# A recurrent layer on one core: R and H of x in one 256-column matmul, outputs in blocks of four pairs

## The chip, the core and the metric

The kernel runs on one core of one Trainium2 chip. A core has TensorE for matmuls, VectorE (DVE), ScalarE (ACT), GpSimd (POOL) and SyncE (SP, which here only starts transfers), and each runs its own list of instructions; semaphores order them. The metric is the device time of one launch in microseconds (us), the median of several runs.

## The reference

A gated recurrent layer over 512 time steps for a batch of 16, with 512 channels, all in fp32, and a residual:

```python
Xz = einsum(X, Wxz) + bxz;  Xr = einsum(X, Wxr) + bxr;  Xh = einsum(X, Wxh) + bxh
def step(H, xs):
    xz, xr, xh = xs
    Z = sigmoid(xz + H @ Whz.T + bhz)
    R = sigmoid(xr + H @ Whr.T + bhr)
    H_tilda = tanh(xh + R * H @ Whh.T + bhh)
    H_new = Z * H + (1.0 - Z) * H_tilda
    Y = H_new @ Whq.T + bhq
    return (H_new, Y)
_, Ys = scan(step, h0, (Xz, Xr, Xh))
return x + transpose(Ys, (1, 0, 2))
```

The flat input x of 16 x 512 x 512 is the sequence, cond_1024 is h0. Each step needs the state of the one before, so the steps can't be done side by side; the parts of x and the outputs Y can be done at any time.

## The kernel before

The steps go in 256 pairs `k`, each with a step `s` = 0 and 1 (the step's number is t = 2k + s). The batch is only 16, so a matmul's stationary side is the state (16 or 32 columns: one or both steps of the pair) and the weights stream past as the moving side, 128 columns in each matmul. TensorE's array is used as four column tiles of 32: tile `j` writes partitions 32j to 32j+31 of a PSUM bank and computes the output channels 128j to 128j+127. The 512 input channels are four parts `m`. So a product of a gate is 4 x 4 = 16 matmuls.

`recur` (L164) is the recurrent product of one gate g (R, Z or H) of one step; it adds onto what the bank `pre[k % 2]` has for that gate, one bank for each of R, Z and H. R and Z take the state, H takes R * state, for which it waits (`reset_ready`, in three parts); R waits for the state (`state_ready`, in three parts). `project_x` (L142) adds the part of x of one gate, for both steps of the next pair, and `project_y` (L153) the output of the pair before, 16 matmuls of 128 columns into `y_bank`. None of the two waits for the running step, so they are put behind Z and behind H, where TensorE would have to wait: they are the filler. The order is written out by hand in the loop at L201: R, Z, 4 matmuls of x's part, H, outputs of the pair before, 12 of x; then for the second step R, Z, 4 of x, H, 28 of x.

ACT fills a bank with the bias ahead of the products (`fill_pre` L232 for the three gates with one copy, `fill_y` L236). DVE transposes the products into the layout of the states (`turn` L267), ACT applies sigmoid or tanh, DVE multiplies and adds: `reset_state` L294, `kept` L299, `fresh` L305, the new `states` L309. After each pair DVE adds the output to the residual in `y_io` (`add_y` L271). SP loads x (`load_xt` L100) and the residual (`load_res` L103) for 8 pairs at a time and stores 8 pairs' outputs (L128), each 512 KB, with two buffers of each. All weights are loaded once, at the start.

Of the kernel before, what the change touches and what calls it, by code (L numbers as in the profile page):

```python
# [13 lines left out]
PAIRS = 8  # L14
TS = 2 * PAIRS
# [8 lines left out]
def gru(nc, x_t, x_res, h0, w_x, w_h, w_q, b_gate, b_out, out):  # L24
    tiles = x_t.shape[0]
    pairs = tiles * PAIRS

    with ExitStack() as ctx:
# [7 lines left out]
        wx = [sb(f"wx{g}", [P, G, C]) for g in range(3)]  # L36
# [4 lines left out]
        bias_out = sb("bias_out", [P, P])  # L41

        xt = sb("xt", [P, 2, PAIRS, G, Q])

        y_io = sb("y_io", [P, 2, PAIRS, P])

        states = sb("states", [P, 2, G, 3 * B])
# [11 lines left out]
        pre = [ctx.enter_context(nc.psum_tensor(f"pre{a}", [P, 3, 512], F32)) for a in range(2)]  # L59
# [3 lines left out]
        wx_loaded = [sem(f"wx_loaded{g}") for g in range(3)]  # L63
        wh_loaded = [sem(f"wh_loaded{g}") for g in range(3)]
        wq_loaded = sem("wq_loaded")
        bias_loaded = sem("bias_loaded")
        bias_ready = sem("bias_ready")
# [26 lines left out]
        def state_of(k, s):  # L94

            return states[:, (k + 1) % 2, :, 2 * B:3 * B] if s == 0 else states[:, k % 2, :, B:2 * B]

        @block.sync
        def _(sp):
            def load_xt(n):  # L100
                sp.dma_start(xt[:, n % 2], x_t[n]).then_inc(xt_loaded[n % 2], 16)

            def load_res(n):  # L103
                sp.dma_start(y_io[:, n % 2], x_res[n]).then_inc(y_loaded[n % 2], 16)

            load_xt(0)
            sp.dma_start(wx[R][:], w_x[R]).then_inc(wx_loaded[R], 16)
            for j in range(G):
                rows = slice(Q * j, Q * (j + 1))
                sp.dma_start(bias_in[rows].rearrange("p a g c -> p (a g c)"),  # L110
                             b_gate[j:j + 1].to_broadcast([Q, 6 * P])).then_inc(bias_loaded, 16)
                sp.dma_start(bias_out[rows], b_out[j:j + 1].to_broadcast([Q, P])).then_inc(bias_loaded, 16)  # L112
            sp.dma_start(wx[Z][:], w_x[Z]).then_inc(wx_loaded[Z], 16)
            sp.dma_start(wx[H][:], w_x[H]).then_inc(wx_loaded[H], 16)
            sp.wait_ge(zeroed, 2)
            sp.dma_start(states[:, 1, :, 2 * B:3 * B], h0).then_inc(h0_loaded, 16)  # L116
# [3 lines left out]
            load_res(0)  # L120
            load_xt(1)
            load_res(1)
            for n in range(tiles):
                if n + 2 < tiles:
                    sp.wait_ge(xt_used, n + 1)
                    load_xt(n + 2)
                sp.wait_ge(y_added, PAIRS * (n + 1))
                sp.dma_start(out[n], y_io[:, n % 2]).then_inc(stored[n % 2], 16)  # L128
                if n + 2 < tiles:
                    sp.wait_ge(stored[n % 2], 16 * (n // 2 + 1))  # L130
                    load_res(n + 2)
            for n in range(2):
                sp.wait_ge(stored[n], 16 * (tiles // 2))
# [7 lines left out]
        def _(pe):  # L141
            def project_x(k, g, first, end):  # L142

                n, tp = divmod(k, PAIRS)
                for m in range(first, end):
                    for j in range(G):
                        mm = nc.tensor.matmul(pre[k % 2][Q * j:Q * (j + 1), g, 0:P], xt[:, n % 2, tp, m, :],  # L147
                                              wx[g][:, m, P * j:P * (j + 1)], start=False, stop=(m == G - 1),
                                              skip_group_check=True)
                if tp == PAIRS - 1 and g == H and end == G:  # L150
                    mm.then_inc(xt_used, 1)

            def project_y(k):  # L153
                if k == 0:
                    pe.wait_ge(wq_loaded, 16)
                pe.wait_ge(y_filled, k + 1)
                for m in range(G):
                    for j in range(G):
                        mm = nc.tensor.matmul(y_bank[k % 2][Q * j:Q * (j + 1), 0:P], states[:, k % 2, m, B:3 * B],  # L159
                                              wq[:, m, P * j:P * (j + 1)], start=False, stop=(m == G - 1),  # L160
                                              skip_group_check=True)
                mm.then_inc(y_projected, 1)

            def recur(g, k, s):  # L164
                t = 2 * k + s
                if t == 0:
                    pe.wait_ge(wh_loaded[g], 16)
                for m in range(G):
# [7 lines left out]
                    else:  # L176
                        of = states[:, (k + 1) % 2, m, 2 * B:3 * B] if s == 0 else states[:, k % 2, m, 0:2 * B]
                    rows = B if s == 0 else 2 * B
                    for j in range(G):
                        mm = nc.tensor.matmul(pre[k % 2][Q * j:Q * j + rows, g, 0:P], of,  # L180
# [5 lines left out]
            pe.wait_ge(zeroed, 2)  # L186
            for a in range(2):
                for j in range(G):
                    for g in range(3):
                        nc.tensor.matmul(pre[a][Q * j:Q * (j + 1), g, 0:P], reset_state[:, 0, :],  # L190
                                         flat(reset_state[:]), start=True, stop=True)
                    mm = nc.tensor.matmul(y_bank[a][Q * j:Q * (j + 1), 0:P], reset_state[:, 0, :],
                                          flat(reset_state[:]), start=True, stop=True)
# [3 lines left out]
            for g in range(3):  # L197
                pe.wait_ge(wx_loaded[g], 16)
                project_x(0, g, 0, G)

            for k in range(pairs):  # L201
                more = k + 1 < pairs
                n, tp = divmod(k + 1, PAIRS)

                recur(R, k, 0)
                recur(Z, k, 0)
                if more:
                    if tp == 0:
                        pe.wait_ge(xt_loaded[n % 2], 16 * (n // 2 + 1))
                    pe.wait_ge(pre_filled, k + 2)  # L210
                    project_x(k + 1, R, 0, 1)
                recur(H, k, 0)
                if k > 0:
                    project_y(k - 1)
                if more:
                    project_x(k + 1, R, 1, G)

                recur(R, k, 1)
                recur(Z, k, 1)
                if more:  # L220
                    project_x(k + 1, Z, 0, 1)
                recur(H, k, 1)
                if more:
                    project_x(k + 1, Z, 1, G)
                    project_x(k + 1, H, 0, G)
            for h in range(N):
                pe.wait_ge(state_ready[h], 2 * pairs + 1)
            project_y(pairs - 1)

        @block.scalar  # L230
        def _(act):
            def fill_pre(k):  # L232

                nc.scalar.copy(pre[k % 2][:, :, 0:P], bias_rows[:]).then_inc(pre_filled, 1)  # L234

            def fill_y(k):  # L236
                if k >= 2:
                    act.wait_ge(y_added, k - 1)
# [131 lines left out]
```

## Time and profile before

| | us |
|---|---|
| median of 3 runs (2446.89 to 2451.39) | 2449.64 |
| the profiled execution | 2457.01 |
| its span | 2455.2 |
| TensorE matmul busy | 2351.4 (96%) |
| TensorE weight load busy | 2230.2 (91%) |
| DVE busy | 1345.5 (55%) |
| ACT busy | 817.1 (33%) |

The mean granted clock of TensorE is 0.998 of full speed (2.4 GHz). A record of TensorE is one row of the trace: each fp32 matmul of the code leaves two matmul records and two weight loads (PEld), 81984 of each. Matmul records overlap, since four column tiles work side by side, so their busy time tells only whether something was running. "L147" is line 147 of the kernel. "Idle before" is the time in which an engine did nothing before a row, with what ended it; "issue" means that nothing in the profile did. Two DMA queues carry instructions: q8 with 640 packets and q14 with 107.

| transfer | times | KB each | us to landing |
|---|---|---|---|
| xt from x | 32 | 512 | 3.4 |
| y_io from the residual | 32 | 512 | 3.3 |
| out from y_io | 32 | 512 | 2.8 |

### The profile page before, as it was taken

The page shows a single profiled execution, that of the slowest core. Times are in us where ns is not written, and L with a number is a line of the kernel's source. Part 1 is how long each engine was busy: PE and PEld are TensorE (multiplying, and loading weights), DVE is VectorE, ACT ScalarE, POOL GpSimd, SP SyncE. Part 2 cuts the span into 40 slices and gives each one's busy share as a digit, 9 for nine tenths or more (in the row PEclk, how much of TensorE's full clock was granted, in tenths as well). Part 3 has the DMA queues.
Part 4 walks back from the last instruction along what each step waited for, and adds up shares of the span by engine and source line. Part 5 has one row for each costly group of instructions (what it writes and reads, how often), then busy time and mean ns, then how long its engine had stood idle before and what let it go on. Part 6 is the DMA issues. An engine that isn't in the chain of part 4 may idle for free.

```text
span 2455.2 us, 177755 instructions
## 1 busy us (share of the span) xinstructions
PE 2351.4 (96%) x81984; PEld 2230.2 (91%) x81984; DVE 1345.5 (55%) x8961; ACT 817.1 (33%) x4610; POOL 0.8 (0%) x6
## 2 busy tenths in 40 slices
PE   8999999999999999999999999999999999999999
PEld 7999989999999999899999899989999898988898
DVE  3555555555555555555555555555555555555555
ACT  2333333333333333333333333333333333333333
POOL 0000000000000000000000000000000000000000
PEclk9999999999999999999999999999999999999999
DMA  4000000000000000000000100000000000000000
GB/s 165 30 22 22 22 30 30 30 13 22 30 30 30 13 30 22 30 30 13 30 22 30 30 23 21 22 30 30 30 13 22 30 30 30 13 22 30 30 13 13
DMA packets 16491, 69.53 MB, mean 28 GB/s; under 512 B 2304, under 2 KB 2432, under 8 KB 14848
## 3 DMA queue, kind: packets, MB, share of 16 engines
q1 hardware_dynamic: 15744, 58.17, 6.7%
q8 instruction: 640, 10.49, 1.8%
q14 instruction: 107, 0.88, 0.1%
HBM read 41.39 MB, written 16.78 MB: 24 GB/s over the span
## 4 chain that ended last, share of the span: by engine, by line
PE 95%; issue 4%; DMA 1%; SPq 0%; DVE 0%; ACT 0%
PE pre L180 57%; PE pre L147 29%; PE y_bank L159 9%; DMA wh<-in_w_hh 1%; SPq L110 0%; SPq L112 0%; DVE pre_t L269 0%; DVE fresh L305 0%; SPq L118 0%; DVE reset_state L294 0%; ACT cand L258 0%; SPq L116 0%; ACT z_not L254 0%; DVE states L309 0%; DVE kept L299 0%
## 5 line engine op out<-in xcount | busy, mean ns | idle before, releaser
L180 PE MATMUL pre<-wh,states 128*16 128x128 f32 x32768 | 1093.4, 273 | 22.7 <-issue 13.4
L147 PE MATMUL pre<-wx,xt 128*32 128x128 f32 x24576 | 1034.6, 273 | 67.9 <-issue 63.7
L269 DVE STREAM_TRANSPOSE pre_t<-pre 128x32 f32<-128x32 f32 (+2 forms) x3584 | 618.4, 216 | 801.8 <-PE pre L180 767.1
L180 PEld LDWEIGHTS pre<-wh,states 128*16 128x16 f32 x32768 | 949.9, 104 | 68.3 <-issue 60.8
L147 PEld LDWEIGHTS pre<-wx,xt 128*32 128x32 f32 x24576 | 814.3, 110 | 120.0 <-issue 117.2
L180 PE MATMUL pre<-wh,reset_state 128*16 128x128 f32 (+1 forms) x16384 | 616.8, 273 | 6.9 <-issue 5.5
L251 ACT ACTIVATE r_gate<-pre_t 128x16 f32<-128x16 f32 (+1 forms) x1536 | 234.5, 215 | 1003.1 <-DVE pre_t L269 1003.1
L180 PEld LDWEIGHTS pre<-wh,reset_state 128*16 128x16 f32 (+1 forms) x16384 | 473.0, 103 | 29.3 <-issue 27.8
L258 ACT ACTIVATE cand<-pre_t 128x16 f32<-128x16 f32 (+1 forms) x1536 | 234.8, 215 | 327.6 <-DVE pre_t L269 327.6
L159 PE MATMUL y_bank<-wq,states 128*32 128x128 f32 x8192 | 299.7, 273 | 1.5 <-DVE states L309 1.5
L159 PEld LDWEIGHTS y_bank<-wq,states 128*32 128x32 f32 x8192 | 258.0, 110 | 1.8 <-DVE states L309 1.8
L299 DVE TENSOR_TENSOR kept<-z_gate,states 128x64 f32<-128x64 f32 x512 | 115.5, 226 | 239.6 <-ACT z_gate L255 239.6
L305 DVE TENSOR_TENSOR fresh<-z_not,cand 128x16 f32<-128x16 f32 (+1 forms) x1536 | 223.1, 181 | 27.2
L294 DVE TENSOR_TENSOR reset_state<-r_gate,states 128x16 f32<-128x16 f32 (+1 forms) x1536 | 222.8, 182 | 27.4
L254 ACT ACTIVATE z_not<-pre_t 128x64 f32<-128x64 f32 x512 | 131.4, 257 | 293.5 <-DVE pre_t L269 293.5
L309 DVE TENSOR_TENSOR states<-fresh,kept 128x16 f32<-128x16 f32 (+1 forms) x1536 | 182.0, 174 | 0.0
L255 ACT ACTIVATE z_gate<-pre_t 128x64 f32<-128x64 f32 x512 | 122.7, 240 | 0.0
L234 ACT COPY pre<-bias_rows 128x384 f32<-128x384 f32 x256 | 120.9, 473 | 0.8 <-DVE bias_rows L280 0.8
L276 DVE TENSOR_TENSOR y_io<-y_bank,y_io 128x128 f32<-128x128 f32 x256 | 72.9, 285 | 1.4 <-PE y_bank L159 1.2
L239 ACT COPY y_bank<-bias_out 128x128 f32<-128x128 f32 x256 | 66.4, 259 | 0.0
L190 PE MATMUL pre<-reset_state 128*32 128x128 f32 x48 | 6.1, 361 | 1.3 <-POOL reset_state L138 1.3
L190 PEld LDWEIGHTS pre<-reset_state 128*32 128x32 f32 x48 | 5.1, 143 | 1.8 <-POOL reset_state L138 1.3
(11 smaller groups left out, 10.5 us busy)
## 6 DMA issues: line engine op xcount, KB each, us to landing
xt<-in_x_t SPq DMA_DIRECT2D x32, 512.0 KB, 3.4
y_io<-in_x_res SPq DMA_DIRECT2D x32, 512.0 KB, 3.3
out<-y_io SPq DMA_DIRECT2D x32, 512.0 KB, 2.8
wx<-in_w_xr SPq DMA_DIRECT2D x1, 1024.0 KB, 5.8
wx<-in_w_xz SPq DMA_DIRECT2D x1, 1024.0 KB, 6.0
wx<-in_w_xh SPq DMA_DIRECT2D x1, 1024.0 KB, 8.2
wh<-in_w_hr SPq DMA_DIRECT2D x1, 1024.0 KB, 11.0
wh<-in_w_hz SPq DMA_DIRECT2D x1, 1024.0 KB, 12.9
```

The lines of the kernel that those rows point to most:

```text
L147: mm = nc.tensor.matmul(pre[k % 2][Q * j:Q * (j + 1), g, 0:P], xt[:, n % 2, tp, m, :], wx[g][:, m, P * j:P * (j + 1)], start=False, stop=( ...
L159: mm = nc.tensor.matmul(y_bank[k % 2][Q * j:Q * (j + 1), 0:P], states[:, k % 2, m, B:3 * B], wq[:, m, P * j:P * (j + 1)], start=False, sto ...
L180: mm = nc.tensor.matmul(pre[k % 2][Q * j:Q * j + rows, g, 0:P], of, wh[g][:, m, P * j:P * (j + 1)], start=False, stop=(m == G - 1), skip_g ...
L234: nc.scalar.copy(pre[k % 2][:, :, 0:P], bias_rows[:]).then_inc(pre_filled, 1)
L251: nc.scalar.activation(r_gate[:, a:b], pre_t[R][:, a:b, mine], ACT.Sigmoid).then_inc(r_ready[h], 1)
L254: nc.scalar.activation(z_not[:], pre_t[Z][:, :, mine], ACT.Sigmoid, scale=-1.0)
L255: nc.scalar.activation(z_gate[:], pre_t[Z][:, :, mine], ACT.Sigmoid).then_inc(z_ready, 1)
L258: nc.scalar.activation(cand[:, a:b], pre_t[H][:, a:b, mine], ACT.Tanh).then_inc(cand_ready[h], 1)
L269: nc.vector.transpose(flat(pre_t[g][:, a:b]), pre[k % 2][:, g, Q * a:Q * b]).then_inc(done, 1)
L294: nc.vector.tensor_tensor(reset_state[:, a:b, B:2 * B], r_gate[:, a:b], old[:, a:b], ALU.mult).then_inc(reset_ready[h], 1)
L305: nc.vector.tensor_tensor(fresh[:, a:b], z_not[:, a:b], cand[:, a:b], ALU.mult).then_inc(fresh_ready[h], 1)
L309: nc.vector.tensor_tensor(new[:, a:b], fresh[:, a:b], kept[:, a:b], ALU.add).then_inc(state_ready[h], 1)
```

## The change

R and H of a pair now share one PSUM bank (`rh_bank`, R in columns 0 to 127 and H in 128 to 255), Z has its own (`z_bank`). `project_rh` computes x's parts of R and H with one matmul of 256 columns where there were two of 128; the weights lie side by side in `wx_rh`. `project_z` is the rest of `project_x`.

Outputs go by blocks of four pairs. `project_y(u, m)` gives each pair of block u a column tile of its own and streams all 512 columns of `wq` past each; in a pair of the next block one of the four parts `m` is done, 4 matmuls of 512 columns. For that `states` is a ring of 8 pairs. In the first four pairs there is no output work, and after the last pair four parts are left. The output add takes 256 columns at a time, in the first two steps of a block, between Z's transpose and `kept`. x, residual and output transfers go by four pairs, 256 KB each; xt's rows in memory are 512 bytes long where they were 4096. ACT fills the gates' banks with two copies, and `y_bank` once in four pairs with 512 columns. The order of the filler is also new, as the loop shows.

```diff
+            for u in range(2):
+                load_res(u)
+            for u in range(blocks):
+
+                if u + 2 < blocks:
+                    sp.wait_ge(xt_used, u + 1)
+                    load_xt(u + 2)
+                if u > 0:
+                    sp.wait_ge(y_added, 2 * u)
+                    sp.dma_start(out[u - 1], y_io[:, (u - 1) % 2]).then_inc(stored[(u - 1) % 2], 16)
+                    if u + 1 < blocks:
+                        sp.wait_ge(stored[(u - 1) % 2], 16 * ((u + 1) // 2))
+                        load_res(u + 1)
+            sp.wait_ge(y_added, 2 * blocks)
+            sp.dma_start(out[blocks - 1], y_io[:, (blocks - 1) % 2]).then_inc(stored[(blocks - 1) % 2], 16)
+            for half in range(2):
+                sp.wait_ge(stored[half], 16 * (blocks // 2))
 
...
-            def project_x(k, g, first, end):
-
-                n, tp = divmod(k, PAIRS)
+            def project_rh(k, first, end):
+
+                u, c = divmod(k, BLOCK)
                 for m in range(first, end):
                     for j in range(G):
-                        mm = nc.tensor.matmul(pre[k % 2][Q * j:Q * (j + 1), g, 0:P], xt[:, n % 2, tp, m, :],
-                                              wx[g][:, m, P * j:P * (j + 1)], start=False, stop=(m == G - 1),
-                                              skip_group_check=True)
-                if tp == PAIRS - 1 and g == H and end == G:
+                        mm = nc.tensor.matmul(rh_bank[k % 2][Q * j:Q * (j + 1), 0:2 * P], xt[:, u % 2, c, m, :],
+                                              wx_rh[:, m, j, :], start=False, stop=(m == G - 1), skip_group_check=True)
+                if end == G and c == BLOCK - 1:
                     mm.then_inc(xt_used, 1)
 
-            def project_y(k):
-                if k == 0:
-                    pe.wait_ge(wq_loaded, 16)
-                pe.wait_ge(y_filled, k + 1)
-                for m in range(G):
+            def project_z(k, first, end):
+                u, c = divmod(k, BLOCK)
+                for m in range(first, end):
                     for j in range(G):
-                        mm = nc.tensor.matmul(y_bank[k % 2][Q * j:Q * (j + 1), 0:P], states[:, k % 2, m, B:3 * B],
-                                              wq[:, m, P * j:P * (j + 1)], start=False, stop=(m == G - 1),
-                                              skip_group_check=True)
-                mm.then_inc(y_projected, 1)
-
-            def recur(g, k, s):
-                t = 2 * k + s
+                        nc.tensor.matmul(z_bank[k % 2][Q * j:Q * (j + 1), 0:P], xt[:, u % 2, c, m, :],
+                                         wx_z[:, m, P * j:P * (j + 1)], start=False, stop=(m == G - 1),
+                                         skip_group_check=True)
+
+            def project_y(u, m):
+
+                if m == 0:
+                    pe.wait_ge(y_filled, u + 1)
+                for c in range(BLOCK):
+                    mm = nc.tensor.matmul(y_bank[u % 2][Q * c:Q * (c + 1), :],
+                                          states[:, (u * BLOCK + c) % RING, m, B:3 * B], wq[:, m, :],
+                                          start=False, stop=(m == G - 1), skip_group_check=True)
+                if m == G - 1:
+                    mm.then_inc(y_projected, 1)
+
+            def recur(g, t):
+                k, s = divmod(t, 2)
...
             for k in range(pairs):
                 more = k + 1 < pairs
-                n, tp = divmod(k + 1, PAIRS)
-
-                recur(R, k, 0)
-                recur(Z, k, 0)
+                u, c = divmod(k, BLOCK)
+                recur(R, 2 * k)
+                recur(Z, 2 * k)
                 if more:
-                    if tp == 0:
-                        pe.wait_ge(xt_loaded[n % 2], 16 * (n // 2 + 1))
+                    if c == BLOCK - 1:
+                        pe.wait_ge(xt_loaded[(u + 1) % 2], 16 * ((u + 1) // 2 + 1))
                     pe.wait_ge(pre_filled, k + 2)
-                    project_x(k + 1, R, 0, 1)
-                recur(H, k, 0)
-                if k > 0:
-                    project_y(k - 1)
+                    project_z(k + 1, 0, 1)
+                recur(H, 2 * k)
+                if u > 0:
+                    if (u, c) == (1, 0):
+                        pe.wait_ge(wq_loaded, 16)
+                    project_y(u - 1, c)
                 if more:
-                    project_x(k + 1, R, 1, G)
-
-                recur(R, k, 1)
-                recur(Z, k, 1)
+                    project_rh(k + 1, 0, 1)
+
+                recur(R, 2 * k + 1)
+                recur(Z, 2 * k + 1)
                 if more:
-                    project_x(k + 1, Z, 0, 1)
-                recur(H, k, 1)
+                    project_z(k + 1, 1, 2)
+                recur(H, 2 * k + 1)
                 if more:
-                    project_x(k + 1, Z, 1, G)
-                    project_x(k + 1, H, 0, G)
+                    project_z(k + 1, 2, G)
+                    project_rh(k + 1, 1, G)
...
-            project_y(pairs - 1)
+            for m in range(G):
+                project_y(blocks - 1, m)
...
             def fill_pre(k):
 
-                nc.scalar.copy(pre[k % 2][:, :, 0:P], bias_rows[:]).then_inc(pre_filled, 1)
-
-            def fill_y(k):
-                if k >= 2:
-                    act.wait_ge(y_added, k - 1)
-                nc.scalar.copy(y_bank[k % 2][:, 0:P], bias_out[:]).then_inc(y_filled, 1)
+                nc.scalar.copy(rh_bank[k % 2][:, 0:2 * P], bias_rows[:, 0:2].rearrange("p g c -> p (g c)"))
+                nc.scalar.copy(z_bank[k % 2][:, 0:P], bias_rows[:, 2]).then_inc(pre_filled, 1)
+
+            def fill_y(u):
+                if u == 0:
+                    act.wait_ge(bias_out_loaded, 16)
+                if u >= 2:
+                    act.wait_ge(y_added, 2 * (u - 1))
+                nc.scalar.copy(y_bank[u % 2][:], bias_out[:]).then_inc(y_filled, 1)
...
+                if s == 1 and k + 2 < pairs:
+                    fill_pre(k + 2)
+                if s == 0 and k % BLOCK == BLOCK - 1:
+                    fill_y(k // BLOCK)
...
+            def add_y(u, half):
+                if half == 0:
+                    dve.wait_ge(y_loaded[u % 2], 16 * (u // 2 + 1))
+                    dve.wait_ge(y_projected, u + 1)
+                cols = slice(half * C // 2, (half + 1) * C // 2)
+                nc.vector.tensor_tensor(y_io[:, u % 2, cols], y_bank[u % 2][:, cols], y_io[:, u % 2, cols], ALU.add
                                         ).then_inc(y_added, 1)
...
+                if t >= 2 * RING and t % RING < 2:
+                    add_y(t // RING - 2, t % RING)
+                dve.wait_ge(z_ready, t + 1)
```

On TensorE, one pair in the steady part of the kernel before (the names are those of the tensors written and read; 16x128 is the stationary columns by the moving ones):

```order
L180 MATMUL pre<-wh,states 16x128 x32
L147 MATMUL pre<-wx,xt 32x128 x4
L180 MATMUL pre<-wh,reset_state 16x128 x16
L159 MATMUL y_bank<-wq,states 32x128 x16
L147 MATMUL pre<-wx,xt 32x128 x12
L180 MATMUL pre<-wh,states 32x128 x32
L147 MATMUL pre<-wx,xt 32x128 x4
L180 MATMUL pre<-wh,reset_state 32x128 x16
L147 MATMUL pre<-wx,xt 32x128 x28
```

and the same place in the changed kernel:

```order
L205 MATMUL rh_bank<-wh,states 16x128 x16
L205 MATMUL z_bank<-wh,states 16x128 x16
L174 MATMUL z_bank<-wx_z,xt 32x128 x4
L205 MATMUL rh_bank<-wh,reset_state 16x128 x16
L183 MATMUL y_bank<-wq,states 32x512 x4
L165 MATMUL rh_bank<-wx_rh,xt 32x256 x4
L205 MATMUL rh_bank<-wh,states 32x128 x16
L205 MATMUL z_bank<-wh,states 32x128 x16
L174 MATMUL z_bank<-wx_z,xt 32x128 x4
L205 MATMUL rh_bank<-wh,reset_state 32x128 x16
L174 MATMUL z_bank<-wx_z,xt 32x128 x8
L165 MATMUL rh_bank<-wx_rh,xt 32x256 x12
```

Between H of the first step and R of the second there were 16 output matmuls and 12 of x, all of 128 columns; now there are 4 of 512 and 4 of 256. Behind H of the second step there were 28 of 128; now there are 8 of 128 and 12 of 256. The 4 matmuls between Z and H are still 4 of 128.

On DVE, in a step of the kernel before, from the R gate on:

```order
L294 TENSOR_TENSOR reset_state<-r_gate,states 128x16 x2
L294 TENSOR_TENSOR reset_state<-r_gate,states 128x2x16
L269 STREAM_TRANSPOSE pre_t<-pre 128x128
L299 TENSOR_TENSOR kept<-z_gate,states 128x64
L269 STREAM_TRANSPOSE pre_t<-pre 128x32 x2
```

and in the first step of a block in the changed kernel:

```order
L323 TENSOR_TENSOR reset_state<-r_gate,states 128x16 x2
L323 TENSOR_TENSOR reset_state<-r_gate,states 128x2x16
L300 STREAM_TRANSPOSE pre_t<-z_bank 128x128
L307 TENSOR_TENSOR y_io<-y_bank,y_io 128x256
L331 TENSOR_TENSOR kept<-z_gate,states 128x64
L300 STREAM_TRANSPOSE pre_t<-rh_bank 128x32 x2
L300 STREAM_TRANSPOSE pre_t<-rh_bank 128x64
L337 TENSOR_TENSOR fresh<-z_not,cand 128x16 x2
```

The output add now stands between Z's transpose and `kept`; it was behind the new state.

## Rows read from the trace of the kernel before

**Rows 1.** the page: busy time by engine, and the chain that ended last.
```profile
PE 2351.4 (96%) x81984; PEld 2230.2 (91%) x81984; DVE 1345.5 (55%) x8961; ACT 817.1 (33%) x4610; POOL 0.8 (0%) x6
...
PE 95%; issue 4%; DMA 1%; SPq 0%; DVE 0%; ACT 0%
```

**Rows 2.** the page: costliest groups; busy us, mean ns of one | idle before.
```profile
L147 PE MATMUL pre<-wx,xt 128*32 128x128 f32 x24576 | 1034.6, 273 | 67.9 <-issue 63.7
```

**Rows 3.** chain of waits, 20 to 40 us: start, duration, what ran.
```profile
8.29 14.88 DMA wh<-in_w_hh
...
29.98 1.75 PE pre L180 x64
```

**Rows 4.** windows view of weight loads: length, busy (count), granted clock, DMA, GB/s.
```profile
20.90:22.61 1.71, 1.42 (x32) 0.50 1.03 431
```

**Rows 5.** windows view of all engines in the steady part.
```profile
25.00:2445.00 2420.00, 2331.03 (x81543) 2214.17 (x81547) 1338.64 (x8921) 810.46 (x4587) 0.00 (x0) 1.00 0.08 25
```

**Rows 6.** waits of the weight loads, 25 to 2445 us: total us, times, longest.
```profile
PEld pre L147 <- issue: 114.2, 209, 2.4
PEld pre L180 <- issue: 88.6, 262, 0.6
```

**Rows 7.** timeline of the weight loads: start, duration, kind, count, idle before.
```profile
2211.46 0.43 PEld L180 LDWEIGHTS pre<-wh,states 128*32 128x32 f32 x16 [0.25 <-issue]
2211.81 0.30 PEld L147 LDWEIGHTS pre<-wx,xt 128*32 128x32 f32 x8
2212.03 0.95 PEld L180 LDWEIGHTS pre<-wh,reset_state 128*32 128x32 f32 x32
2212.90 1.61 PEld L147 LDWEIGHTS pre<-wx,xt 128*32 128x32 f32 x56
2214.43 0.50 PEld L180 LDWEIGHTS pre<-wh,states 128*16 128x16 f32 x16
2215.20 1.29 PEld L180 LDWEIGHTS pre<-wh,states 128*16 128x16 f32 x48 [0.27 <-issue]
...
2220.31 0.47 PEld L147 LDWEIGHTS pre<-wx,xt 128*32 128x32 f32 x17 [1.69 <-issue]
```

**Rows 8.** instruction queue; GB/s in 40 slices, 2208 to 2212, then 2216 to 2222.
```profile
q8 instruction: 640, 10.49, 1.8%
...
GB/s 0 0 0 0 0 0 0 0 164 0 0 0 0 0 0 0 0 0 0 0 0 0 0 0 0 0 0 0 0 0 0 0 0 0 0 0 0 0 0 0
...
GB/s 109 218 246 437 382 410 328 410 382 273 28 27 109 0 0 0 0 0 0 0 0 0 0 0 0 0 0 0 0 0 0 0 0 0 0 0 109 0 0 0
```

**Rows 9.** timeline of all engines at pair 0, where TensorE ran out of filler.
```profile
24.09 0.84 PE L147 MATMUL pre<-wx,xt 128*32 128x128 f32 x24
...
25.19 0.36 DVE L309 TENSOR_TENSOR states<-fresh,kept 128x16 f32<-128x16 f32 x3
...
25.41 0.42 PE L180 MATMUL pre<-wh,states 128*32 128x128 f32 x8 [0.48 <-DVE states L309]
```

**Rows 10.** timeline of all engines in a pair of the steady part.
```profile
2226.82 0.46 ACT L251 ACTIVATE r_gate<-pre_t 128x16 f32<-128x16 f32 x3 [1.82 <-DVE pre_t L269]
...
2228.23 0.23 DVE L299 TENSOR_TENSOR kept<-z_gate,states 128x64 f32<-128x64 f32 x1 [0.47 <-ACT z_gate L255]
2228.23 1.14 PE L159 MATMUL y_bank<-wq,states 128*32 128x128 f32 x32
...
2229.39 0.36 DVE L309 TENSOR_TENSOR states<-fresh,kept 128x16 f32<-128x16 f32 x3
...
2229.76 0.51 PE L180 MATMUL pre<-wh,states 128*32 128x128 f32 x11
```

**Rows 11.** the page: the output add and the bias fill of the gates.
```profile
L234 ACT COPY pre<-bias_rows 128x384 f32<-128x384 f32 x256 | 120.9, 473 | 0.8 <-DVE bias_rows L280 0.8
L276 DVE TENSOR_TENSOR y_io<-y_bank,y_io 128x128 f32<-128x128 f32 x256 | 72.9, 285 | 1.4 <-PE y_bank L159 1.2
```

**Rows 12.** the page: DMA issues; count, KB each, us to landing.
```profile
xt<-in_x_t SPq DMA_DIRECT2D x32, 512.0 KB, 3.4
```

More of the change, by code:

```diff
@@ L21, with gru @@
 N = len(PARTS)
-def gru(nc, x_t, x_res, h0, w_x, w_h, w_q, b_gate, b_out, out):
-    tiles = x_t.shape[0]
-    pairs = tiles * PAIRS
+BLOCK = 4
+RING = 2 * BLOCK
+def gru(nc, x_t, x_res, h0, w_xrh, w_xz, w_h, w_q, b_gate, b_out, out):
+    pairs = x_t.shape[0]
+    blocks = pairs // BLOCK
     with ExitStack() as ctx:
@@ L33, in sem @@
             return ctx.enter_context(nc.semaphore(name))
-        wx = [sb(f"wx{g}", [P, G, C]) for g in range(3)]
+        wx_rh = sb("wx_rh", [P, G, G, 2 * P])
+        wx_z = sb("wx_z", [P, G, C])
         wh = [sb(f"wh{g}", [P, G, C]) for g in range(3)]
@@ L40, in gru @@
         bias_rows = sb("bias_rows", [P, 3, P])
[L41 to L47, printed above, removed]
+        bias_out = sb("bias_out", [P, C])
+        xt = sb("xt", [P, 2, BLOCK, G, Q])
+        y_io = sb("y_io", [P, 2, C])
+        states = sb("states", [P, RING, G, 3 * B])
         reset_state = sb("reset_state", [P, G, 2 * B])
@@ L119, in _ @@
             sp.dma_start(wq[:], w_q).then_inc(wq_loaded, 16)
-            load_res(0)
+            sp.dma_start(bias_out[:], b_out.to_broadcast([P, C])).then_inc(bias_out_loaded, 16)
             load_xt(1)
[L122 to L133, printed above, removed]
+            for u in range(2):
[14 more added lines that the diff above has]
+                sp.wait_ge(stored[half], 16 * (blocks // 2))
         @block.gpsimd
@@ L166, in recur @@
+            def recur(g, t):
+                k, s = divmod(t, 2)
                 if t == 0:
@@ L316 @@
+            for u in (blocks - 2, blocks - 1):
+                for half in range(2):
+                    add_y(u, half)
 _W = "L0_cond_"
@@ L326 @@
     batch, steps, chans = x.shape
-    tiles = steps // TS
+    pairs = steps // 2
     def by_block(v):
@@ L362 @@
         a[name] = nc.dram_tensor(f"in_{name}", v.shape, _mybir.dt.from_np(v.dtype), kind="ExternalInput").ap()
-    out = nc.dram_tensor("out", (tiles, P, PAIRS, P), _mybir.dt.float32, kind="ExternalOutput").ap()
-    gru(nc, a["x_t"], a["x_res"], a["h0"], [a["w_x" + g] for g in "rzh"], [a["w_h" + g] for g in "rzh"], a["w_q"],
+    out = nc.dram_tensor("out", (pairs // BLOCK, P, C), _mybir.dt.float32, kind="ExternalOutput").ap()
+    gru(nc, a["x_t"], a["x_res"], a["h0"], a["w_xrh"], a["w_xz"], [a["w_h" + g] for g in "rzh"], a["w_q"],
         a["b_gate"], a["b_out"], out)
     r = _run(nc, [arrays], core_ids=[0])
-    y = _np.asarray(r.results[0]["out"]).reshape(tiles, G, 2, batch, PAIRS, P)
-    return _np.ascontiguousarray(y.transpose(3, 0, 4, 2, 1, 5)).reshape(batch, steps, chans)
+    y = _np.asarray(r.results[0]["out"]).reshape(steps, batch, chans)
+    return _np.ascontiguousarray(y.transpose(1, 0, 2))
```

174 lines of the change are left out of this document (82 added, 92 removed).

## The prediction

> **What bounds the kernel now.** I read the page's first and fourth part first. TensorE is busy for 96% of the span and the chain of waits runs through it for 95%; the other engines stay at 55% or less [rows 1]. So what counts is what fills TensorE, and whether all of that is work. The costliest groups give each matmul record 273 ns [rows 2], which can't be its price, since 81984 of them would be 22 ms: four column tiles work side by side. The chain of waits has the price: in a stretch without any gap 64 records take 1.75 us, 27.3 ns each, 109.4 ns for one on each of the four tiles [rows 3]. (Every fp32 matmul of the code is two records, and each record has a weight load beside it.) The time goes with the columns streamed: while the granted clock was 0.50 (1.2 GHz), 32 loads took 1.71 us, 53.4 ns each [rows 4]. Twice the stream at half the clock, 213.8 ns for four, means 106.9 ns of stream at 2.4 GHz and 2.5 ns of something fixed per batch of four records.
>
> Then the windows view of the steady part: from 25 to 2445 us there are 81543 records [rows 5]. At 27.34 ns they are 2229 us, and the window is 2420. **190 us are not work.** The waits name them: TensorE's weight loads sat idle in 471 places, 203 us, for "issue", that is for nothing the profile shows [rows 6]. (An idle load counts some 0.03 us more than the matmuls lose.) The timeline of the loads shows their rhythm: between the idle of 2211.46 and that of 2215.20 lie 16+8+32+56+16 = 128 loads, 256 instructions with their matmuls [rows 7]. The page has an instruction queue with 640 packets and 10.49 MB, 16 KB each [rows 8], and 81984 records and as many loads are 640.5 times 256 instructions. So TensorE's program is fetched block by block, and it runs dry at the block's end. The packet for the idle that ended at 2211.46 started at 2208.8 [rows 8]: 2.6 us from fetch to first instruction, in which the engine had 2.6 - 0.25 = 2.35 us of work left, 84 to 86 records. A fetch is asked for when about 84 records remain; they stream 84 x 27.3 = 2.30 us; what is missing to 2.6 is the stall. The long ones are those whose fetch meets a data transfer: xt's burst fills the DMA engines from 2216 to 2217.6, the packet gets out at 2217.8, and the loads stand for 1.69 us [rows 7, 8].
>
> The Trainium skill has a rule here ("Runtime: NRT & Kernel Launch", section "Instruction fetch mechanics"): instructions come in 16 KiB blocks of 256, and the cost of crossing a boundary is mostly hidden. The trace agrees with the block and not with the hiding: 0.25 us of idle at such a boundary [rows 7]. By the rule the fetch terms below would be zero, which is my third rival.
>
> **The change, part by part** (against the profiled run, 2457.0 us; the median of the plain runs is 2449.6, 7 less).
>
> *Streaming.* The columns stay the same. R and H of x: 32 matmuls of 128 columns become 16 of 256, 16 batches of records become 8; each saves one fixed 2.5 ns, 20 ns a pair. Outputs: 8 batches become 2 of 512 columns, 15 ns. 35 ns x 256 = 9 us. Bounds: 0 (a wide matmul has its own price) and -18 (double the fixed part). I take -9.
>
> *Blocks fetched.* A pair issued 160 matmuls, now 132: 320 records become 264, and 640 blocks about 529.
>
> *Cover of each fetch.* The 84 records ahead of a boundary used to be 2.30 us wherever it fell. Now an output record streams 107.5 ns (+80) and an RH record 54 (+27). In the order of a pair, 264 records, outputs and the first RH part stand at 104 to 119 (+0.64 and +0.21 us), the other RH part at 240 to 263 (+0.64). A boundary is covered when some 0.3 us of that lies in its last 84 records: positions 108 to 193 and 251 to 73 of the next pair, 171 of 264. Exposed are 93 of 264, 35%. Today's plain stalls: about 410 x 0.25 = 102 us (0.16 a block over 640). Afterwards 529 x 0.35 x 0.16 = 30. Term -70. Bounds: -102 (none left) and -17 (only the count falls, 111 x 0.16).
>
> *Fetches that meet transfers.* 190 - 102 - 4 leaves 84 us in the long stalls; there are 64 bursts (32 of xt, 32 of out with the next residual), 1.3 us each. The bytes stay, but transfers go from 512 KB to 256 KB and twice as often [rows 12]. A burst half as long holds a fetch half as long, and two thirds of the fetches have 0.3 to 0.85 us to spare. Halving alone (twice as many, a quarter of the damage each) gives 42; xt's packets shrink to 512 B, which no row prices, so I take 49: -35. Bounds -70 and +84 (each burst costs 1.3 us as now).
>
> *A shorter filler between H and the next R.* This speaks against the change. After H of a pair's first step TensorE needs the new state. In pair 0, where it ran out of filler, the first filler record started at 24.09 and R at 25.41: the chain takes 1.32 us, plus some 0.02 since the first weights load uncovered [rows 9]. In the steady state the filler is 32 output and 24 x records, 2228.23 to 2229.76, 1.53 us [rows 10]; it just hides the chain. Afterwards it is two output batches (0.860) and two RH batches (0.433), 1.29 us. That misses 0.03 + 0.02 where the tiles are level, and up to 0.14 where one lags by most of a batch (the last state add starts 1.16 us after the filler in [rows 10], 1.10 in [rows 9]). 252 pairs give 13 to 35 us; most pairs begin level because this wait levels them, so I take +18. After the second step the filler grows from 1.53 to 1.73 us and stays hidden.
>
> *Pairs 1 to 3* have no output work now: filler 0.43, missing 0.89 each, and pair 0 misses 0.22 more than its 0.66: +3 us. Their streaming returns at the end, where it always cost the same.
>
> *What I cost at nothing.* DVE's add of 256 columns (0.285 us for 128 [rows 11], so about 0.42) now stands between Z's transpose and `kept`, where DVE idles 0.47 us for ACT [rows 10]; if it outgrew that, H's transposes would be up to 0.1 us late in 126 of 512 steps, 6 us with half of them on the path. ACT's fill of R, H and Z is two instructions (0.47 [rows 11] becomes about 0.63) and that of y 512 columns (about 0.6 every fourth pair); ACT idles 1.82 us before R's gates [rows 10]. Priming has 56 matmuls for 32; the weights land at 23 us (the piece that begins at 8.29 and takes 14.88 [rows 3]), which covers it, and losing that cover is 2 us. SP's stores wait for blocks that are whole pairs away from being needed.
>
> Sum: -9 - 70 - 35 + 18 + 3 = -93. 2457.0 - 93 = 2364 for the profiled run, 2449.6 - 93 = **2357 us** for the median, 3.8% faster.
>
> **Rivals.**
> 1. *Only the count falls.* If a fetch is asked for by time, or the wide records shorten the lookahead (fewer than 84 wait in the queues), no cover is gained. -9 - 17, long stalls by their count -15, +21: -20, 2430 us. For it: all records of today last equally long, so no row tells records from time. Against it: queues hold instructions, and the distance in [rows 7, 8] fits one number.
> 2. *Slower: transfers hold fetches up.* 128 bursts at 1.3 us are 168, 84 more. -9 - 70 + 84 + 21 = +26: 2476. Place: SP's xt, store and residual transfers. It decides from 1.1 us per burst, where the rest of the gain is used up. For it: today nearly every burst has a long stall to its name. Against it: half the bytes per burst.
> 3. *The rule is right and the idle has another cause* that stays: -9 + 21 = +12, 2462. Against it stand the 128 loads and the 16 KB.
> 4. *The filler's lack is worse* (0.14 us in every pair, +35): still 2374, inside the first case.
>
> **How the numbers follow.** Forecast 0.64 (its own range 2325 to 2395), rival 1 0.21, rival 2 0.08, rival 3 0.03; 0.04 lies between them near no change. About 0.2% (5 us) is what can be told from no change. Faster: 0.64 + 0.21 + 0.01 = 0.86; same 0.03; slower 0.11. The range from 2325 to 2440 takes in the forecast and rival 1 and leaves out 0.16.
>
> **What would show it.** 529 packets in the instruction queue. "Issue" idle of the loads near 80 us in some 200 to 250 places, none of the plain ones where the last 84 records hold outputs. A new wait of R's loads for the states (fresh, kept), 0.05 us or so each, in each first step. 64 RH records in 3.46 us. If the issue idle stays above 150 us, my cover is wrong; if the wait for states exceeds 40 us, the filler term is; if long stalls are as long as now and twice as many, rival 2 holds.

## The result and the profile after

The changed kernel takes 2273.38 us (median of 4 runs, 2272.9 to 2273.59), the kernel before 2449.99 in the same comparison: a ratio of 0.928 (95% interval 0.9264 to 0.9297). That is 176.6 us or 7.2% faster. The forecast was 2357 us, the range 2325 to 2440: right in its sign and wrong in its size, by nearly half of the gain.

The page of the changed kernel has the parts that stood in [rows 1] and [rows 8]: busy time by engine, the chain that ended last, and the instruction queue (packets, MB, share of the DMA engines).

```profile
PE 2256.5 (99%) x67696; PEld 1879.4 (83%) x67696; DVE 1328.1 (58%) x8833; ACT 827.6 (36%) x4674; POOL 1.7 (0%) x6
...
q8 instruction: 529, 8.67, 1.6%
...
PE 98%; DMA 1%; DVE 0%; SPq 0%; issue 0%; ACT 0%; DVEq 0%
```

The 529 packets came as forecast, and "issue" fell from 4% of the chain to 0. TensorE's busy share rose to 99%: its work is hardly shorter (see the rates below), the stretches without work are gone. The waits of the weight loads from 25 to 2265 us, as in [rows 6]:

```profile
PEld rh_bank L165 <- issue: 150.2, 502, 0.3
PEld rh_bank L205 <- DVE states L344: 89.9, 258, 1.2
```

The first of these rows reads like the old stalls and is none. It is on rh's loads alone, never over 0.3 us, two in each pair, and each stands behind 512-column records of the outputs: four loads of 110 ns are followed by the next four only when the tiles have streamed their 512 columns, 0.43 us. In e3 below, which has the outputs 128 wide and rh's matmuls as here, this idle is gone (0.3 us in all). In the matmuls nothing is missing, as the timeline of TensorE over one pair shows (start, duration, what ran; a group's duration includes the last record's full length):

```profile
1005.03 1.04 PE L183 MATMUL y_bank<-wq,states 128*32 128x512 f32 x8
1005.89 0.61 PE L165 MATMUL rh_bank<-wx_rh,xt 128*32 128x256 f32 x8
1006.35 1.08 PE L205 MATMUL rh_bank<-wh,states 128*32 128x128 f32 x32
1007.25 1.06 PE L205 MATMUL z_bank<-wh,states 128*32 128x128 f32 x32
...
1009.65 1.48 PE L165 MATMUL rh_bank<-wx_rh,xt 128*32 128x256 f32 x24
1010.94 1.06 PE L205 MATMUL rh_bank<-wh,states 128*16 128x128 f32 x32
...
1013.78 1.04 PE L183 MATMUL y_bank<-wq,states 128*32 128x512 f32 x8
```

From output to output is 8.75 us. The eight output records start 0.86 us before rh's, the 24 of rh 1.29 us before R's: just the columns at 106.9 ns for 128, and the small fixed part of 2.5 ns a batch. The group at 1006.35 is 1.08 long where its like take 1.06, and rh's eight records take 0.46 for their 0.43; these 0.05 to 0.06 us are the forecast wait for the state. All else is stream: 8.75 is 8.70 of stream (e7 below measures it without the wait) and 0.05 of waiting, in nearly every pair. Before, 81543 records filled 2420 us [rows 5], 9.50 us for the 320 of a pair, some 8.74 of them stream.

The new wait stands in the timeline of all engines, with DVE's add as in [rows 10]:

```profile
1004.97 0.23 DVE L331 TENSOR_TENSOR kept<-z_gate,states 128x64 f32<-128x64 f32 x1 [0.16 <-ACT z_gate L287]
...
1006.13 0.35 DVE L344 TENSOR_TENSOR states<-fresh,kept 128x16 f32<-128x16 f32 x3
1006.35 0.26 PEld L205 LDWEIGHTS rh_bank<-wh,states 128*32 128x32 f32 x11 [0.33 <-DVE states L344]
```

The add of 256 columns left DVE 0.16 us before `kept` and hurt nothing.

### The profile page after: what moved, and what is told of

The parts are those of the page before. It is cut to its first block, busy times and chain, and to the rows that moved or that the text cites. A ratio compares the mean times of both kernels' runs of the same rounds, so it can differ in the third digit from the quotient of the medians.

```text
span 2271.7 us, 149519 instructions
## 1 busy us (share of the span) xinstructions
PE 2256.5 (99%) x67696; PEld 1879.4 (83%) x67696; DVE 1328.1 (58%) x8833; ACT 827.6 (36%) x4674; POOL 1.7 (0%) x6
## 4 chain that ended last, share of the span: by engine, by line
PE 98%; DMA 1%; DVE 0%; SPq 0%; issue 0%; ACT 0%; DVEq 0%
PE rh_bank L205 40%; PE z_bank L205 20%; PE rh_bank L165 19%; PE z_bank L174 10%; PE y_bank L183 10%; DMA wh<-in_w_hh 1%; DVE fresh L337 0%; DVE pre_t L300 0%; SPq L125 0%; ACT cand L290 0%; SPq L131 0%; DVE states L344 0%; SPq L129 0%; SPq L123 0%; SPq L116 0%
## 5 line engine op out<-in xcount | busy, mean ns | idle before, releaser
L300 DVE STREAM_TRANSPOSE pre_t<-rh_bank 128x32 f32<-128x32 f32 (+1 forms) x3072 | 455.8, 200 | 666.6 <-PE rh_bank L205 625.6
L205 PE MATMUL rh_bank<-wh,states 128*16 128x128 f32 (+1 forms) x16384 | 547.6, 274 | 3.3 <-DVE states L344 3.3
L205 PEld LDWEIGHTS rh_bank<-wh,states 128*16 128x16 f32 (+1 forms) x16384 | 435.4, 103 | 137.1 <-DVE states L344 89.9
L205 PE MATMUL rh_bank<-wh,reset_state 128*16 128x128 f32 (+1 forms) x16384 | 541.1, 273 | 1.2 <-DMA wh<-in_w_hh 1.2
L205 PE MATMUL z_bank<-wh,states 128*16 128x128 f32 (+1 forms) x16384 | 541.1, 273 | 0.0
L165 PE MATMUL rh_bank<-wx_rh,xt 128*32 128x256 f32 x8192 | 537.0, 380 | 2.1 <-issue 2.1
L205 PEld LDWEIGHTS rh_bank<-wh,reset_state 128*16 128x16 f32 (+1 forms) x16384 | 454.2, 103 | 1.9 <-DMA wh<-in_w_hh 1.5
L205 PEld LDWEIGHTS z_bank<-wh,states 128*16 128x16 f32 (+1 forms) x16384 | 454.4, 103 | 0.3 <-DMA wh<-in_w_hz 0.3
L174 PE MATMUL z_bank<-wx_z,xt 128*32 128x128 f32 x8192 | 364.4, 273 | 0.0
L183 PE MATMUL y_bank<-wq,states 128*32 128x512 f32 x2048 | 266.0, 592 | 1.5 <-DVE states L344 1.5
```

Of the source, the lines that this page charges most:

```text
L165: mm = nc.tensor.matmul(rh_bank[k % 2][Q * j:Q * (j + 1), 0:2 * P], xt[:, u % 2, c, m, :], wx_rh[:, m, j, :], start=False, stop=(m == G - ...
L174: nc.tensor.matmul(z_bank[k % 2][Q * j:Q * (j + 1), 0:P], xt[:, u % 2, c, m, :], wx_z[:, m, P * j:P * (j + 1)], start=False, stop=(m == G ...
L183: mm = nc.tensor.matmul(y_bank[u % 2][Q * c:Q * (c + 1), :], states[:, (u * BLOCK + c) % RING, m, B:3 * B], wq[:, m, :], start=False, stop ...
L205: mm = nc.tensor.matmul(gate_bank(g, k % 2)[Q * j:Q * j + rows], of, wh[g][:, m, P * j:P * (j + 1)], start=False, stop=(m == G - 1), skip_ ...
L300: nc.vector.transpose(flat(pre_t[g][:, a:b]), gate_bank(g, t // 2 % 2)[:, Q * a:Q * b]).then_inc(done, 1)
```

## The experiments

After the result three theories stood. A "record" is, as before, one matmul row of the trace with its weight load, and 128 records are a block of 256 instructions. **A, supply:** a block can't be had more often than once in about 3.73 us, the median distance between two fetches before; 128 records streamed in 3.50, so TensorE starved at all times, and whoever takes longer than 3.73 us for a block never starves. **B, the prediction's cover:** a fetch is asked for a fixed 84 records ahead, and what counts is what these 84 stream. **C:** the gain is not from the instructions at all but from smaller transfers, the shared bank or the new order.

**e1: everything 128 columns wide again**, blocks, ring, bank and transfers as in the change.

```diff
-                for c in range(BLOCK):
-                    mm = nc.tensor.matmul(y_bank[u % 2][Q * c:Q * (c + 1), :],
-                                          states[:, (u * BLOCK + c) % RING, m, B:3 * B], wq[:, m, :],
+                for q in range(4):
+                    cols = slice(P * q, P * (q + 1))
+                    for c in range(BLOCK):
+                        mm = nc.tensor.matmul(y_bank[u % 2][Q * c:Q * (c + 1), cols],
+                                              states[:, (u * BLOCK + c) % RING, m, B:3 * B], wq[:, m, cols],
```

and rh's in two halves of 128 in the same way.

> The changed kernel with every matmul 128 columns wide again: rh's as two of 128, the outputs' as four of 128. A pair has 320 records again; block order, ring, transfers of four pairs and filler stay. Theory A (supply: a block of 256 instructions can't be had more often than once in about 3.73 us, the median time between fetches before, while 128 records stream in 3.50 us): stalls come back at every block, 2.5 blocks a pair x 3.73 = 9.33 us a pair, 2388 + 25 for start and end + transfers' stalls 10 to 40: 2420 to 2455. Theory B (the prediction's: fetch 84 records ahead, a stall where these stream in under 2.6 us): no wide records, so as before, 2430 to 2460. Theory C (the gain came from the smaller transfers, the shared bank or the order, not from the number of instructions): stays near 2280.

2427.4 us, 0.9921 of before (0.9891 to 0.9951). Nearly all of the gain is gone: C falls for all but 20 us. A and B both wanted about this time, so e1 doesn't part them. Its steady part, 25 to 2400 us (length, loads busy and their count, granted clock, DMA, GB/s):

```profile
25.00:2400.00 2375.00, 2206.72 (x81005) 1.00 0.09 25
```

2375 / 81005 x 128 = 3.75 us a block.

**e2 and e3: only rh, or only the outputs, split to 128.** 296 and 288 records a pair.

> Only rh's matmuls split into two of 128; outputs stay 512 wide. 296 records a pair, 2.31 blocks. A: 2.31 x 3.73 = 8.63 us a pair is under the 8.78 that it streams and waits, so almost no stalls but those of transfers: 2275 to 2300. B: only the 8 output records give cover, about 70% of 592 blocks stay exposed at 0.16 us = 66 us, and 45 for transfers: 2370 to 2400. C: 2275 to 2285.

> Only the outputs' matmuls split into four of 128; rh's stay 256 wide. 288 records a pair, 2.25 blocks. A: 2.25 x 3.73 = 8.39 us a pair, under its stream: 2273 to 2290. B: about 60% of 576 blocks exposed, 55 us, and 45 for transfers: 2350 to 2390. C: 2275 to 2285.

2294.2 us (0.9382, 0.9352 to 0.9411) and 2276.0 us (0.9304, 0.9279 to 0.9328). B wanted 2350 to 2400 for both and falls; A's 2275 to 2300 and 2273 to 2290 hold. The gain is not a sum of parts. Either half of the change alone has most of it: rh's merge 2276, the wide outputs 2294, both 2273, none 2427. At 288 records a block lasts 3.9 us, at 296 3.8, just above the supply's period, where some stalls are left.

**e4: 28 matmuls of 4 columns more in each pair**, wide ones untouched; they write a spare bank and their output is unused.

```diff
+            def tiny(n):
+                for _ in range(n):
+                    for j in range(G):
+                        nc.tensor.matmul(spare[Q * j:Q * (j + 1), 0:4], reset_state[:, 0, :], wq[:, 0, 0:4],
+                                         start=True, stop=True)
```

> The changed kernel with its wide matmuls, and 28 matmuls of 4 columns added in each pair (12 behind the first rh part, 16 behind the last), into a spare bank: 320 records a pair again, their output unused. They stream 0.05 us a pair by columns; if each record costs a weight load's time, up to 0.2 to 0.8 us. A: 2.5 x 3.73 = 9.33 us a pair at least: 2410 to 2450. B: wide records still cover two thirds of the blocks, 640 x 0.35 x 0.16 = 36 and 45 for transfers: 2340 to 2370 and what the tiny ones cost by themselves. C: 2285 and what they cost.

2423.9 us (0.9909, 0.988 to 0.9937), the time of e1 within 0.2%, though it streams hardly more columns than the change: 150 us for instructions that compute next to nothing. Its steady part has the same price by the record, 2375 / 80922 x 128 = 3.76 us a block:

```profile
25.00:2400.00 2375.00, 2141.62 (x80922) 1.00 0.09 25
```

But not all of these 150 us are the supply. This is TensorE over one of the shortest pairs:

```profile
1074.16 1.07 PE L185 MATMUL y_bank<-wq,states 128*32 128x512 f32 x8
...
1075.45 0.35 PE L194 MATMUL spare<-wq,reset_state 128*32 128x4 f32 x22
...
1080.21 0.43 PE L194 MATMUL spare<-wq,reset_state 128*32 128x4 f32 x30
...
1083.32 0.64 PE L185 MATMUL y_bank<-wq,states 128*32 128x512 f32 x4
```

From output to output is 9.16 us without a stall, 0.4 more than the change's 8.75. So the 56 added records cost 0.4 us a pair by themselves, some 7 ns each, whatever their columns: about 100 of the 150 us. The other 50 are stalls (the loads' idle for "issue", other than that behind the wide outputs, is 39 us in 88 places here and 144 us in 364 in e1). A price of its own for each instruction is thus a rival that stood in none of the three theories, and e4 can't exclude it; A's floor of 9.33 us a pair and this 9.16 lie too close. e5 parts them.

**e5: the supply by itself** (one run). Behind the last output stand stretches of 1536 records, 12 blocks each, of 32 to 256 columns; they write a spare bank and their output is unused.

```diff
+            for cols in (32, 64, 96, 112, 128, 136, 144, 160, 256):
+                for _ in range(192):
+                    for j in range(G):
+                        nc.tensor.matmul(spare[Q * j:Q * (j + 1), 0:cols], reset_state[:, 0, :], wq[:, 0, 0:cols],
+                                         start=True, stop=True)
```

> The changed kernel with nine stretches of 768 matmuls (1536 records, 12 blocks) behind its last output, into a spare bank, the four column tiles in turn: 32, 64, 96, 112, 128, 136, 144, 160, 256 columns. Their output is unused. A: a floor of 3.5 to 3.75 us a block, 27.3 to 29.3 ns a record, in the stretches up to 128 columns, and the columns' own time (30.7 x columns/144 ns a record) from 144 on. B: no floor; every stretch pays the same 0.25 us or so a block on top of its stream down to the narrow ones, where 84 records no longer last: at 64 columns 84 records stream in 1.2 us, so 1.4 us of stall a block, 3.2 us a block. C says nothing here.

The windows view of the loads, one row for each of the stretches from 32 to 160 columns (length, loads busy and count, granted clock, DMA, GB/s):

```profile
2266.52:2307.27 40.75, 19.86 (x1535) 0.58 0.04 11
2307.28:2352.52 45.24, 23.93 (x1547) 0.93 0.02 4
2352.53:2396.68 44.15, 31.54 (x1542) 1.00 0.02 4
2396.69:2441.59 44.90, 36.35 (x1543) 1.00 0.02 5
2441.59:2486.41 44.82, 41.30 (x1542) 1.00 0.02 4
2486.42:2531.09 44.67, 44.24 (x1540) 1.00 0.02 4
2531.09:2578.13 47.04, 47.04 (x1539) 1.00 0.02 4
2578.13:2630.29 52.16, 52.16 (x1539) 1.00 0.02 4
```

From 64 to 136 columns the time is the same within 2.5%, 3.68 to 3.77 us a block, whatever is streamed, where B wanted 3.2 us at 64 columns; at 144 it is the stream's own 3.92 and at 160 its 4.35. (The 32-column stretch found its first block loaded: 11 blocks in 40.75 us, 3.70 each.) Below the bend time goes by instructions, above it by columns. The bend lies where 128 records stream in 3.7 us, at 136 columns; the kernel before sat at 128, barely on the wrong side.

What makes the period can be read there too. First the timeline of the loads in the 32-column stretch (start, duration, count, idle before), then the DMA view of 2280 to 2290 us, whose 40 slices are 0.25 us each:

```profile
2281.20 1.80 PEld L265 LDWEIGHTS spare<-wq,reset_state 128*32 128x32 f32 x128 [1.67 <-issue]
2284.68 1.80 PEld L265 LDWEIGHTS spare<-wq,reset_state 128*32 128x32 f32 x128 [1.67 <-issue]
2288.69 1.80 PEld L265 LDWEIGHTS spare<-wq,reset_state 128*32 128x32 f32 x128 [2.22 <-issue]
2292.44 1.80 PEld L265 LDWEIGHTS spare<-wq,reset_state 128*32 128x32 f32 x128 [1.95 <-issue]
```

```profile
GB/s 0 0 0 0 0 0 0 0 0 66 0 0 0 0 0 0 0 0 0 0 0 0 0 66 0 0 0 0 0 0 0 0 0 0 0 0 0 0 0 66
```

Blocks begin at 2281.20, 2284.68, 2288.69 and 2292.44, each of 128 loads that need 1.80 us, with no load for 1.7 to 2.2 us before each. An even price for every instruction would spread that idle over all records; here it comes once in 128. The distances are 3.48, 4.01 and 3.75 us, and no starved block of these stretches has another (within 0.02 us): the 3.7 us are a mean of three steps. Fetches start in the slices at 2282.25 and 2285.75: 1.1 to 1.3 us after a block began, and 2.2 to 2.9 before the next one began. The same two views in the 128-column stretch, now 2450 to 2470 us with slices of 0.5 us:

```profile
2451.36 3.43 PEld L265 LDWEIGHTS spare<-wq,reset_state 128*32 128x32 f32 x128 [0.57 <-issue]
2455.11 3.43 PEld L265 LDWEIGHTS spare<-wq,reset_state 128*32 128x32 f32 x128 [0.32 <-issue]
```

```profile
GB/s 0 0 0 0 0 33 0 0 0 0 0 0 33 0 0 0 0 0 0 0 33 0 0 0 0 0 0 0 33 0 0 0 0 0 0 33 0 0 0 0
```

The fetches at 2452.5 and 2456.0 again come 0.9 to 1.6 us after the block's beginning (1.1 in both by the unrounded records), though the 128 loads take nearly twice as long here, 3.43 us for 1.80. So a starved TensorE asks for the next block about 1.1 us into the one just come and has it 2.2 to 2.9 us after that, 3.7 in all. In records these 1.1 to 1.2 us are 40 to 44 at 128 columns (which leaves the prediction's 84 or a few more) and about 80 at 32 columns, where fewer than 50 are left. B's constant was no constant.

**e6: the kernel before with 144 columns** in its x and recurrent matmuls, 16 of them into unused columns: the same instructions, more work.

```diff
-                                              wh[g][:, m, P * j:P * (j + 1)], start=False, stop=(m == G - 1),
+                                              wh[g][:, C * m + P * j:C * m + P * j + WIDE], start=False, stop=(m == G - 1),
```

> The kernel before with all x and recurrent matmuls 144 columns wide, 16 of them into unused columns (288 of 320 records a pair): the same instructions, 12% more columns, 9.70 us of stream a pair instead of 8.74. A: 128 records now stream in 3.88 us, more than 3.73: the plain stalls go, and the fetches get some lead over the transfers: 2483 + 25 + 0 to 40 = 2510 to 2550, only 3 to 4% more than before. B: 84 records stream in 2.55 us, 0.05 short: nearly the same, 2530 to 2570, but the long stalls stay as they are, +84. If the stalls had another cause they stay: 2483 + 190 + 25 = 2700.

The x matmuls are widened in the same way. 2514.4 us (1.0242, 1.0209 to 1.0274): 12% more columns in nine tenths of the matmuls cost 2.4%. The waits of the loads for "issue", 203 us in 471 places before [rows 6], are down to 5.6 in 9:

```profile
PEld pre L151 <- issue: 5.4, 8, 1.2
PEld pre L184 <- DVE states L313: 0.7, 1, 0.7
PEld pre L184 <- issue: 0.2, 1, 0.2
```

This kernel has before's big transfers, all its instructions and no cover by wide records, and it has hardly any stalls, long ones included. B wanted 2530 to 2570 us with the long stalls as before. That settles A against B, and it shows that the transfers hurt a supply without a lead and hardly one that has it.

**e7: more filler where it is missing.** One 128-column part of z goes from behind the second H to behind the first.

```diff
                     project_rh(k + 1, 0, 1)
+                    project_z(k + 1, 1, 2)
...
-                    project_z(k + 1, 1, 2)
+                    project_z(k + 1, 2, 3)
                 recur(H, 2 * k + 1)
                 if more:
-                    project_z(k + 1, 2, G)
+                    project_z(k + 1, 3, G)
```

> The changed kernel with one 128-column part of z moved from behind the second step's H to behind the first step's H. The wait for the states in front of the second step's R (60 ns a pair in its trace) should go: 1.51 us of filler for a chain of 1.41; behind the second H 1.51 us are left. 252 x 0.06 = 15 us: 2258. If the chain moves along with it, nothing.

2257.95 us (0.9198 of before, 0.9172 to 0.9224; 2257.16 to 2258.97 in 6 runs, all below the change's lowest 2272.9). The wait for the states is gone from the steady part, 89.9 us of idle loads in 258 places down to (25 to 2240 us; the change has 88.0 in 255 there):

```profile
PEld rh_bank L165 <- issue: 150.2, 502, 0.3
PEld rh_bank L205 <- DVE states L345: 3.3, 5, 0.8
```

TensorE from output to output, 8.70 us where the change has 8.75:

```profile
1006.63 1.04 PE L183 MATMUL y_bank<-wq,states 128*32 128x512 f32 x8
...
1015.33 0.61 PE L183 MATMUL y_bank<-wq,states 128*32 128x512 f32 x4
```

It is the fastest version, and the filler term is measured by it: 15.4 us between the two medians, which stem from different comparisons, and some 14 us by the traces (57 ns between the median pairs, 252 times). The 89.9 us of idle loads were worth no more: an idle of 0.33 us in front of R's loads cost the matmuls 0.06.

**e8: the kernel before with transfers of 256 KB**, to price them.

```diff
-PAIRS = 8
+PAIRS = 4
```

> The kernel before with PAIRS = 4: x, residual and outputs move 4 pairs at a time, 256 KB in each transfer and twice as many; instructions and columns stay. It prices the transfers alone. Before takes 3.80 us a block in its steady part, e1_all128, with 256 KB transfers and the same number of records, 3.75. Theory A with transfers that hold a fetch up by their length: about 3.75 here too, 637 blocks x 0.05 = 30 us less, 2415 to 2435. If every burst costs as much as now (the prediction's slower rival): 2510 to 2540. If the sizes of transfers don't matter and e1's 20 us came from its bank or order: 2445 to 2460.

2413.9 us where before took 2425.6 (0.9955, 0.9938 to 0.9973). Before runs 24 us faster in this comparison than in the result's, so only the ratio counts: 0.45%, some 11 us for halved transfers, against A's 30 and the slower rival's loss. Of e1's 20 us some 9 stay unexplained. e1 to e4, e5 to e7 and e8 ran on three different chips; whether that is why before differs was not tried.

## Why the prediction was right in its sign and wrong in its size

- *What bounds the kernel.* Right: the columns' stream, and 190 us in which TensorE waits for its own instructions, in blocks of 256. e5 and e6 show it directly. The third rival, by which the idle would stay, is refuted, and with it the Trainium skill's sentence ("Runtime: NRT & Kernel Launch", "Instruction fetch mechanics") that crossing a block's boundary is mostly hidden: it is hidden above 3.7 us a block and not below.
- *Streaming, -9.* Holds as far as it can be read: 0.86 us for the output records and 1.29 for the last 24 of rh are the columns and 2.5 ns a batch. The way to the 2.5 ns was not sound: halving the 213.8 ns of the slow clock takes for granted that the fixed part is nothing there, which no row shows; with the same fixed part at both clocks the rows would give 104.4 and 5.0. The changed kernel's 429 ns for a batch of 512 columns against 109.4 for 128 give 106.5 ns for each 128 columns and some 3 fixed, and so bear the forecast out.
- *Blocks fetched.* 529 as worked out.
- **The step that failed: "A fetch is asked for when about 84 records remain", and the term -70 built on it.** It took a time in a starved state, the 1.1 us that pass before the next request, for a count of records. (In the changed kernel a fetch starts some 120 records ahead of a boundary, by the median of fetches and records counted in the traces.) With a fixed distance only wide records within the last 84 could help, and 35% of the blocks stayed exposed. What the runs show in its place is a supply with a period of 1.1 + 2.6 = 3.7 us. It is a second rate beside the stream's 3.50 us a block, and the slower of the two sets the time: 640 x (3.73 - 3.50) = 147 us for the period alone. After the change a pair lasts 8.75 us and has 264 / 128 = 2.06 blocks, 4.2 us each; the supply gets a lead, and every plain stall goes, wherever its boundary falls. e2, e3 and e6 show that the place of the wide records doesn't matter.
- *Fetches that meet transfers, -35.* The same error. A held-up fetch costs only where there is no lead, so nearly all of this term went (e6: 5.6 us of stalls left with the old transfers). With the -102 and -84 that I had as the plain and the long stalls, the sum would have been -9 - 102 - 84 + 18 + 3 = -174; measured are 176.6. The first was my outer bound of its term, the second lay beyond the bound of -70; and the range ended at 2325, which left both together out, though one cause removes both.
- *Filler, +18.* Right in mechanism and near in size: 15.4 us by e7, with nearly every pair the same length, as level tiles would give.
- *The edits at nothing* were nothing: DVE kept 0.16 us before `kept`.
- *Rivals.* The first (only the count falls) and the second (more transfers, more holds) both described a starved supply, which the change ended. The first had the condition right, a request by time; what it drew from that, that nothing is gained, was wrong.
- *The signs.* Two were badly chosen. "Issue" idle above 150 us was to say that the cover is wrong; it is wrong, but the 151 us say nothing of it: nearly all of them stand behind the wide outputs, where they cost nothing. A wait for the states above 40 us was to refute the filler term; there are 90 us, of which the matmuls lose 15. Both counted idle loads where only idle matmuls cost time.

Left open: whether the 1.1 us are a fixed time or that in which a certain part of a block is handed out, and what the 2.6 us consist of, and why the period comes in three steps. That the 1.1 us are the same at 32 and at 128 columns speaks for a fixed time.

## What to carry to other kernels

Where an engine's instructions are many and short, work out the time per block of instructions from the count, not only the time per column: here, below 3.7 us for 256 TensorE instructions (29 ns for a matmul record with its load, of which each fp32 matmul of the code has two) time goes by instructions. Merging a few matmuls until the average is above that gives nearly all of the gain at once (3.8 us a block left 21 us, 3.9 left 3), and more merging next to nothing. Idle stretches that come every 256 instructions with no releaser are the sign; a distance read in a starved state must not be taken for what holds once the starving ends. And where fillers get fewer or wider, compare what is left of them with the chain they hide: 0.06 us in 252 places were 15 us, back by moving one group.

## What the runs showed of the hardware

- The supply's period doesn't depend on TensorE's clock or on the columns: in e5's 32-column stretch, where the engine idled about half of the time, the granted clock averaged 0.58 of full speed, at 64 columns 0.93, and a block still took 3.70 and 3.77 us.
- The 56 records of 4 columns that e4 adds to a pair take 0.4 us without any stall, some 7 ns each, where their columns at 106.9 ns for 4 x 128 would be under 1 ns; and each takes as much of the supply as one of 512 columns, since a block has 256 instructions whatever they do (639 packets in e4 for its 81808 records).
- In e5 starved blocks came 3.47, 3.75 or 4.02 us apart and at no other distance; the next fetch started 1.1 us into a block at 32 and at 128 columns alike.
- Four column tiles stream 128, 256 and 512 fp32 columns at one rate: 0.86 us for eight records of 512.
